# Second expert layer: rows scattered into slot order, expert matrices as moving side

## The reference, cut to what matters

```python
x = x + ffn(_layernorm(x))
# ffn, on xt = the normed tokens, 2048 x 128
logits = xt @ router_w.T                       # 8 experts
topk_vals, topk_idx = top_k(logits, 2)
g = sigmoid(topk_vals); g = g / (g.sum(-1, keepdims=True) + 1e-10)
for e in range(8):
    ge = sum(where(topk_idx == e, g, 0), -1)
    h = silu(xt @ w_gate[e]) * (xt @ w_up[e])  # 128 -> 256
    out = out + ge[:, None] * (h @ w_down[e])  # 256 -> 128
```

## Time and profile before

| | us |
|---|---|
| median of 3 executions | 437.59 |
| lowest, highest | 434.67, 439.3 |
| the profiled execution, first to last instruction (its span) | 501.4 |
| in it: start of kernel to the first gather of layer one | 54.6 |
| second layer: `slot` ready to first gather | 14.1 |
| second layer: first gather to the landing of the last scatter | 135 |

### The profile page before, as it was taken

One profiled execution on the slowest core, in us unless ns is written; L12 is line 12 of the kernel. 1 busy time (PEld: TensorE's weight loads), 2 busy tenths in 40 slices (PEclk: granted clock), 3 DMA queues, 4 the chain that ended last, 5 costly groups with the idle time before them and its releaser, 6 DMA issues. The chain is left out here.

```text
span 501.4 us, 8428 instructions
## 1 busy us (share of the span) xinstructions
PE 332.9 (66%) x2020; PEld 300.6 (60%) x2020; DVE 251.3 (50%) x890; ACT 207.0 (41%) x940; POOL 261.6 (52%) x273
## 2 busy tenths in 40 slices
PE   2669498797987878768887730723666767665630
PEld 2668387696976768668787720622556656655520
DVE  4969546544445656455565726569222322222217
ACT  4449276634445564465565501500322322232210
POOL 5996434555465466655765561302455556556530
PEclk9999899967689889898899955555787887888885
DMA  4780423222232223222342116110444443344536
GB/s 106 250 256 41 151 65 129 76 75 74 74 122 100 74 74 117 93 86 74 78 133 86 43 33 168 42 42 38 174 140 167 156 169 136 136 157 168 137 120 190
DMA packets 34694, 57.04 MB, mean 114 GB/s; under 512 B 5792, under 2 KB 21088, under 8 KB 34416
## 3 DMA queue, kind: packets, MB, share of 16 engines
q1 hardware_dynamic: 29040, 45.41, 25.3%
q0 software_dynamic: 5440, 11.15, 8.9%
q10 hardware_dynamic: 192, 0.23, 0.1%
HBM read 17.39 MB, written 8.72 MB: 52 GB/s over the span
## 5 line engine op out<-in xcount | busy, mean ns | idle before, releaser
L526 POOL DMA_INDIRECT xg<-xrows,gi x85 | 84.6, 995 | 73.1 <-issue 22.5
L538 POOL DMA_INDIRECT yrows<-yb,si x85 | 84.1, 989 | 30.0 <-issue 24.6
L549 POOL TENSOR_TENSOR rh<-c2ve,neghalf 128x8 f32<-128x8 f32 x23 | 45.8, 1991 | 77.8 <-DVE c2ve L1189 77.8
L873 PE MATMUL bank<-ident,xg 128*128 128x128 f32 x85 | 26.2, 356 | 68.9 <-DMA xg<-xrows,gi 40.5
L884 PE MATMUL bank<-wbuf,x1T 128*128 128x128 f32 x340 | 59.2, 315 | 15.6 <-DVE x1T L1239 7.8
L1236 DVE SCALAR_TENSOR_TENSOR wraw<-xn,bank 128x256 f32<-128x256 f32 x39 | 16.4, 420 | 93.9 <-ACT xn L736 66.9
L976 PE MATMUL bank<-xT,wbuf 128*128 128x128 f32 x312 | 55.8, 336 | 8.6 <-ACT xT L726 8.4
L884 PEld LDWEIGHTS bank<-wbuf,x1T 128*128 128x128 f32 x340 | 50.3, 220 | 18.6 <-issue 9.8
L892 PE MATMUL bank<-xT,wbuf 128*128 128x256 f32 x184 | 58.4, 447 | 0.5 <-ACT xT L665 0.5
L976 PEld LDWEIGHTS bank<-xT,wbuf 128*128 128x128 f32 x312 | 50.8, 247 | 11.1 <-ACT xT L726 5.2
L873 PEld LDWEIGHTS bank<-ident,xg 128*128 128x128 f32 x85 | 12.5, 172 | 74.2 <-issue 43.2
(11 more groups left out here) (180 smaller groups left out, 726.5 us busy)
## 6 DMA issues: line engine op xcount, KB each, us to landing
wbuf<-rec SPq DMA_DIRECT2D x39, 384.0 KB
wbuf<-rec SPq DMA_DIRECT2D x23, 523.0 KB
blocks<-yrows SPq DMA_DIRECT2D x8, 512.0 KB, 6.6
wbuf<-wd SPq DMA_DIRECT2D x23, 128.0 KB
wraw<-in_L_attn_w_up SPq DMA_DIRECT2D x1, 2048.0 KB, 18.5
xg<-xrows,gi POOLq DMA_INDIRECT x85
yrows<-yb,si POOLq DMA_INDIRECT x85
x<-in_L_attn_hidden_states SPq DMA_DIRECT2D x4, 256.0 KB, 4.5
```

Of the source, the lines that this page charges most:

```text
L526: g.indirect_dma_start(rows, None, xrows[l], bass.IndirectOffsetOnAxis(ap=index, axis=0)).then_inc(s_gath[l][b], 16)
L538: g.indirect_dma_start(yrows[l], bass.IndirectOffsetOnAxis(ap=index, axis=0), rows, None).then_inc(s_scat[l][b], 16)
L549: g.tensor_tensor(rh[:], c2ve[:], neghalf[:, 0:HV * NH].rearrange("p (h k) -> p h k", h=HV), ALU.pow).then_inc(s_rh, 1)
L873: ins = t.transpose(dst[:, h * P:(h + 1) * P], xg2[:, b * n + h, :], ident[:])
```

## The change

- While the first layer is being prepared, SP fills a new DRAM tensor `xslots` (39 * 128 rows of 129 words): 128 zero words and in the last word a spare destination row, different for each slot.
- The one-hot part of `route(1)` is gone. GpSimd scatters the normed rows of `x1`, now 129 words wide with the pair's number as last word, straight to their slots: 16 columns for each of 2 experts, 32 indirect DMAs.
- When all 32 have landed, SP loads tiles of 128 consecutive slots by plain DMAs into a ring of 8. The destination rows of a tile's result are the last word of the loaded rows, so no `gidx`, `sidx`, `gi2` or `si2` is used.
- The expert record is not copied. TensorE loads the expert's number into a register (twice a tile, once for gate and up, once for down) and reads `rec2` at that address as the moving side: one matmul of 512 columns for gate and up. The output has the tokens on the partitions, so before the down product the hidden tile must be turned (two transposes, and a copy by ScalarE, `hT2`).
- The loop is written out in full (44 steps) rather than a hardware loop.

```diff
+R2I, R2G, R2H, R2Y = 8, 3, 3, 4
+N2 = LNT[1]
...
# sync, before the store of xn to xrows
+            sp.wait_ge(s_fid, 2)
+            xsv = xslots.rearrange("(j p) d -> p j d", p=P)
+            sp.dma_start(xsv[:, :, 0:D], zrow[:].unsqueeze(1).to_broadcast([P, N2, D])).then_inc(s_fill, 16)
+            sp.dma_start(xsv[:, :, D:D + 1].bitcast(U32), fid[:].unsqueeze(2), allow_slow_non_contiguous=True).then_inc(s_fill, 16)
...
# sync, second layer
+            for k in range(TOPK):
+                for q in range(4):
+                    sp.wait_ge(s_disp[k][q], 64)
...
+            for j in range(N2):
+                if j >= R2I:
+                    sp.wait_ge(s_xtp[1], j - R2I + 1)
+                    sp.wait_ge(s_scat2[(j - R2I) % R2Y], 16 * ((j - R2I) // R2Y + 1))
+                sp.dma_start(xin2[:, j % R2I, :], xslots[j * P:(j + 1) * P, :]).then_inc(s_in2[j % R2I], 16)
...
# gpsimd, constants
+            g.memset(zrow[:], 0.0).then_inc(s_fid, 1)
+            g.iota(fid[:], pattern=[[P, N2]], base=PAIRS, channel_multiplier=1).then_inc(s_fid, 1)
+            for k in range(TOPK):
+                g.iota(pid[:, k, :], pattern=[[TOPK, TT]], base=k, channel_multiplier=TOPK * TT).then_inc(s_id1, 1)
...
# gpsimd, second layer
+            pool.wait_ge(s_slot, 1)
+            pool.wait_ge(s_x1[1], 4)
+            pool.wait_ge(s_fill, 32)
+            for k in range(TOPK):
+                for i in range(TT):
+                    if i % 4 == 0:
+                        pool.wait_ge(s_id1, TOPK + 1 + k * (i // 4 + 1))
+                    c = TOPK * i + k
+                    g.indirect_dma_start(
+                        xslots, bass.IndirectOffsetOnAxis(ap=slotu[:, c:c + 1], axis=0), x1[:, i, :], None)\
+                        .then_inc(s_disp[k][i // 4], 16)
+            for j in range(N2):
+                pool.wait_ge(s_yb[1], j + 1)
+                pool.wait_ge(s_in2[j % R2I], 16 * (j // R2I + 1))
+                g.indirect_dma_start(
+                    yrows[1], bass.IndirectOffsetOnAxis(ap=xin2[:, j % R2I, D:D + 1].bitcast(U32), axis=0),
+                    yb2[:, j % R2Y, :], None).then_inc(s_scat2[j % R2Y], 16)
...
# scalar: per step, xT2 of tile s+2, hT2 of s-2, tanh of s, yb2 of s-3; the last after
+                    act.wait_ge(s_y[1], j + 1)
+                    if j >= R2Y:
+                        act.wait_ge(s_scat2[j % R2Y], 16 * (j // R2Y))
+                    a.activation(yb2[:, j % R2Y, :], Y2, ACT.Copy).then_inc(s_yb[1], 1)
...
# tensor
+            def loop2(s):
+
+                if 0 <= s + 2 < N2:
+                    j = s + 2
+                    pe.wait_ge(s_in2[j % R2I], 16 * (j // R2I + 1))
+                    at_least(pe, s_xts[1], j - 1)
+                    t.transpose(XT2[j % 2], xin2[:, j % R2I, 0:D], ident[:]).then_inc(s_xtp[1], 1)
+                if 0 <= s < N2:
+                    pe.wait_ge(s_xts[1], s + 1)
+                    at_least(pe, s_hh, s - R2G + 1)
+                    e = pe.value_load(expert[1][0:1, s:s + 1], min_val=0, max_val=E - 1)
+                    t.matmul(GU2[s % R2G], xT2[:, s % R2Y, :],
+                             rec2[:, bass.ds(e, 1), GATE:GATE + 2 * I].rearrange("p a n -> p (a n)"),
+                             start=True, stop=True).then_inc(s_g, 1)
+                if 0 <= s - 2 < N2:
+                    j = s - 2
+                    pe.wait_ge(s_hh, j + 1)
+                    at_least(pe, s_hts, j - 1)
+                    for c in range(CH):
+                        ins = t.transpose(HT2[j % 2][:, c * P:(c + 1) * P], hh2[:, j % R2H, c * P:(c + 1) * P], ident[:])
+                    ins.then_inc(s_htp, 1)
+                if 0 <= s - 3 < N2:
+                    j = s - 3
+                    pe.wait_ge(s_hts, j + 1)
+                    at_least(pe, s_yb[1], j)
+                    e = pe.value_load(expert[1][0:1, j:j + 1], min_val=0, max_val=E - 1)
+                    for c in range(CH):
+                        ins = t.matmul(Y2, hT2[:, j % R2H, c * P:(c + 1) * P],
+                                       rec2[:, bass.ds(e, 1), DOWN + c * D:DOWN + (c + 1) * D].rearrange("p a n -> p (a n)"),
+                                       start=(c == 0), stop=(c == CH - 1))
+                    ins.then_inc(s_y[1], 1)
```

More of the change, by code:

```diff
@@ L126, in program @@
         hif = sb("hif", [P, TT * TOPK])
+        slotu = sb("slotu", [P, TT * TOPK], U32)
         cmpj = sb("cmpj", [1, LNT[1] + 1, E])
@@ L135, in program @@
         pairi = sb("pairi", [P, NA], U32)
-        gidx = [sb(f"gidx{l}", [P, NA], U32) for l in range(2)]
-        sidx = [sb(f"sidx{l}", [P, NA], U32) for l in range(2)]
+        gidx = [sb("gidx", [P, NA], U32)]
+        sidx = [sb("sidx", [P, NA], U32)]
         ex = sb("ex", [P, TT, TOPK])
@@ L370, in load_pairs @@
             def load_pairs(l):
-                for b in range(WAYS[l]):
-                    sp.wait_ge(s_scat[l][b], 16 * (LTS[l] // P) * ((LNT[l] - b + WAYS[l] - 1) // WAYS[l]))
+                ring, scat = ((WAYS[0], s_scat[0]), (R2Y, s_scat2))[l]
+                for b in range(ring):
+                    sp.wait_ge(scat[b], 16 * (LTS[l] // P) * ((LNT[l] - b + ring - 1) // ring))
                 yv = yrows[l][0:PAIRS, :].rearrange("(p m) d -> p m d", p=P)
@@ L526, in gather @@
                     g.indirect_dma_start(
-                        rows, None, xrows[l], bass.IndirectOffsetOnAxis(ap=index, axis=0)).then_inc(s_gath[l][b], 16)
+                        rows, None, xrows, bass.IndirectOffsetOnAxis(ap=index, axis=0)).then_inc(s_gath[l][b], 16)
             def scatter(l, u, b):
@@ L557, in _ @@
                 norms(0, quarter(c), s_rstd[1])
-            pool.wait_ge(s_used, 2)
-            paired(g)
-            for b in range(3):
-                gather(1, 0, b)
-            def step2(u, b):
-                gather(1, *earlier(1, u, b, -3))
-                scatter(1, *earlier(1, u, b, 2))
-            steps(pool, step2, 1, 2)
+            pool.wait_ge(s_slot, 1)
[15 more added lines that the diff above has]
+                    yb2[:, j % R2Y, :], None).then_inc(s_scat2[j % R2Y], 16)
         @block.scalar
@@ L745, in _ @@
+            for s in range(-2, N2 + 3):
+                loop2(s)
         @block.tensor
@@ L1061, in route @@
                         ins.then_inc(s_hot[l], 1)
[L1063 to L1067 removed]
+                experts(l)
                 dve.wait_ge(s_perm[l], 1)
@@ L1228, in _ @@
             route(1)
-            def step2(u, b):
-                if not active(1, u, b):
-                    return
-                j = 4 * u + b
-                both = bank[4 + b][:].rearrange("p (g c t) -> p g c t", g=2, c=CH)
+            for j in range(N2):
+                b = j % R2G
                 dve.wait_ge(s_thg, j + 1)
-                v.scalar_tensor_tensor(gg2[:, b], th2[:, b], 1.0, both[:, 0], ALU.add, ALU.mult).then_inc(s_gg, 1)
+                v.scalar_tensor_tensor(gg2[:, b], th2[:, b], 1.0, GU2[b][:, 0:I], ALU.add, ALU.mult).then_inc(s_gg, 1)
                 dve.wait_ge(s_gg, j + 1)
-                at_least(dve, s_y[1], j - 3)
-                v.tensor_tensor(hh2[:, b], both[:, 1], gg2[:, b], ALU.mult).then_inc(s_hh, 1)
-            steps(dve, step2, 1, 0)
+                at_least(dve, s_htp, j - R2H + 1)
+                v.tensor_tensor(hh2[:, j % R2H], GU2[b][:, I:2 * I], gg2[:, b], ALU.mult).then_inc(s_hh, 1)
             for c in range(4):
```

175 lines of the change are left out of this document (83 added, 92 removed).

## The result

The changed kernel takes 471.21 us (median of 6, 466.15 to 473.63), the kernel before 437.23 us (6 runs, 434.67 to 439.76) in the same session. The ratio is 1.0747, 95% interval 1.0677 to 1.0816: 34 us slower, where 440.4 was forecast and 464 was the upper end. The profiled execution of the changed kernel took 466.15 us, with a span of 464.4; it is the quickest of the six. On some chips every execution of these kernels is held by short stops, and the trace on which the prediction rests is of that sort (span 501.4), while the timed runs of both kernels are of the other, here called ordinary.

A forecast was written before the change was run, and what follows sets the result against it. A circle of waits was taken to hold the second layer's loop. The loop gains 32 us, the dispatch takes it back, the start adds 1.6: span +3.2 us, scaled by 0.87 to +2.8, giving 440.4 us; range 424 to 464.

The forecast's parts named there:

- the scale of 0.87: Last step of the sum: the profiled span's +3.2 us times 0.87 gives +2.8 us, 440.4 us.
- the fills: At the start: zero rows 10.2 us plus single words 2.5 us, against 11.5 us of free queue: +1.2 us.
- The circle of waits: Old second-layer loop: six indirect DMAs, last landing, then ScalarE's list hold it at 3.42 us a tile; floor 2.54.
- fills in the way: Rival at the start: words go out on one engine, store of `xn` up to 39 us later, 474 us; chance 0.07.
- The three constants: At the start: GpSimd writes three more small constants before `s_const`, all on the path: +0.4 us.
- The dispatch: Before the second loop: 32 serial scatters at 1.27 us, landing and first load; the loop begins some 28 us later.
- The rival of 1.6 us a scatter: Before the second loop: the queue limits the 32 scatters, 10 us more, 450 us; chance 0.08.
- TensorE's step: New second-layer loop: TensorE's work for one tile takes 2.0 us, or 2.7 with an exposed register load.
- The ring: New second-layer loop: row buffer reuse makes three periods one step plus 5.5 us; 2.6 us a tile taken.
- The quicker ring: Rival in the new loop: faster load, register loads hidden, 2.25 us a tile, 428 us; chance 0.25.
- The slow TensorE: Rival in the new loop: lower clock or both register loads exposed, step 3.6 to 3.9 us, 459 us; chance 0.20.
- The instruction fetch: Old second-layer loop: a 5.25 us stop fits a taken branch's forced fetch; the written-out loop would have none.

The follow-up runs named there:

- after_b: The changed kernel with no edit, run on a chip with the stops: 521.5 us against 514.42 for the kernel before, ratio 1.0157.
- hybrid_b: The changed kernel's compute loop with the old indirect gathers, ring of 16, no fills or dispatch; on chips with stops 503.45 and 503.23 us in two runs.

## Why the prediction was wrong

**The failed step: the scale of 0.87.** The prediction saw that its trace (span 501.4) was 64 us over the median, and wrote "Scaled by 0.87", as if each stage shrank alike. Its last sentence named the danger, that an ordinary execution shortens the old loop and not the serial dispatch, and said that one profile couldn't show it. This is what happened: from the last scatter of layer one to the last of layer two before takes 184.1 us in the trace read and 159.8 in an ordinary one; after takes 184.1 where 185.7 was worked out. The error of the whole sum on the new side is 1.6 us, on the old side 24.3. On the chips with stops the sum came out: +3.2 us were worked out there, +7.1 measured (ratio 1.0033 to 1.0282), and from the last scatter of layer one on, after_b takes 184.7 us where the three traces of before take 184.1 to 185.9; the rest is the fills. The scale took a surplus that the same trace put down to `remote` in two loops, 41 and 6.8 us of it, and spread it over everything.

It was also the answer to "what bounds the kernel now". The circle of waits with 2.87 us of idle GpSimd was there, but only in that sort of execution. In the ordinary one the loop is bound by GpSimd at 2.56 us a tile, which the prediction named as the floor. "So the loop gains 0.8 us a tile" became 0.1 (2.56 to 2.47).

**The fills** were mis-sized: +1.2 us was taken, 6.7 measured by the medians (7.5 to 9.2 at the first gather). The zero rows were priced at the 251 GB/s of the earlier trace rows, 10.2 us; they landed after 24.3 us, which is 105 GB/s, beside the words, whose issue alone held SP's queue for 12.56 us where 2.5 of work were assumed. Where the earlier trace rows has the DMA engines idle from 36.5 to 48, they now move 172 GB/s from 36 to 48 and 119 from 48 to 60, and the words land at 59.3. The rival (fills in the way) was right in kind, at a sixth of its 39 us; that its 474 us lie near the measured time is chance.

**The three constants** (four by the diff, with the zero row), +0.4 us, can't be seen: without early fills the first gather starts between 53.7 and 57.3 us in the traces of either kernel.

**The dispatch** was right: 32 scatters at 1.27 (1.265), landing 2.24 (2.29), SP's issue 0.14 after it (340.43 - 340.28 = 0.15), load 2.5 (1.91). The rival of 1.6 us a scatter is out. TensorE's first work lies 80.9 us behind the last scatter of layer one, 82.9 were worked out.

**TensorE's step** was given as 2.0 us, or 2.7 with an exposed register load. With two loads it is 2.21 and without any 1.60. The 2.0 had hidden loads in it: without loads it was too high by 0.4, and the loads that it put at nothing cost 0.61, so the two errors cancelled in part, which is luck. The 2.7 charged one load with 0.7; two cost 0.61.

**The ring** was right in kind and nearly in size: (step + 5.5) / 3 with the measured step of 2.21 is 2.57, measured 2.47; the value taken was 2.6. With the measured load (1.91, near the 2.0 of the quicker ring) and landing the 5.5 are 5.0 and the formula gives 2.40. The quicker ring's 2.25 didn't come, as its step of 1.8 had the loads at nothing. That the ring and not the step is the bound is shown by the ring of 16, in which the period falls to the step's 2.21.

**The slow TensorE** didn't come: the clock is 0.95 in the new loop, 0.65 in its first 7.6 us, behind the dispatch at 0.50, and 0.98 from 350 us on. By the Trainium skill (TensorE: Matmul & The Clock Gate, Part 1), a TensorE that waits between bursts falls back to half clock, and the prediction left open whether the new loop's short waits would do. In this trace they don't: short waits are in the new loop in nearly every step (0.52 us before L1014). Behind the long wait of the dispatch it does agree.

**The instruction fetch.** The 5.25 us stop was put beside the rule of the Trainium skill (Runtime: NRT & Kernel Launch, Instruction fetch mechanics), that straight code is fetched ahead. No run bears this out as the cause: on a chip without stops the looped code of before has no such stop in its chain, and on a chip with stops the written-out loop with gathers (hybrid_b) still has 8.9 us of them under ScalarE's copy of the result. What the written-out loop of the changed kernel lacks is more than the branch, so the rule is neither shown nor refuted, but the stops go with the chip and with the gathers, not with the form of the loop.

**The chances.** Slower had 0.45, the direction with the most weight, but as a mixture of rivals none of which is what happened: that the direction came true is no merit of the working.

## What to carry to other kernels

If the profiled execution is longer than the timed ones, don't scale it: look in the list of waits of the whole span for releasers that are nothing of the kernel, and in which stage they lie, ask of each wait whether it would survive in a shorter execution, and cost the change once with the loop as read and once with it at its floor. A change that keeps the floor can't gain more than the loop's distance from it; one that removes it, as here the gathers, is bounded by the next engine. The serial stage on GpSimd was paid in full on both sorts of chip (39.2 us from its first scatter to its last). And a register load in TensorE's queue was cheapest behind a long matmul that is already issued, once for each tile; its cost shows in the period and only in part in the idle rows, so measure it by replacing it with a constant.

## What the runs showed that was not expected

**Two sorts of chips.** The kernel before took 514 to 516 us on two chips and 436 to 438 on three others, each execution within 3% of its chip's median. On the first two the waits list the `remote` releaser that the ordinary traces don't have; of the changed kernel there (after_b):

```profile
DVE h L1275 <- remote: 25.1, 14, 3.1
ACT pre L706 <- remote: 12.8, 7, 2.5
DVE nig L1207 <- remote: 6.9, 2, 3.7
```

Its traces on the other chips have none. The granted clock is also lower there (0.79 over the span of before, against 0.89 on an ordinary chip), but a stop needs no fall: from 100 to 120 us of after_b the clock was full, and yet

```profile
102.93 0.48 DVE L1275 SCALAR_TENSOR_TENSOR h<-bank,onib,wraw 128x256 f32<-128x256 f32 x1 [2.43 <-remote]
```

The stops fall in loops with gathers (the first layer of every kernel, the second of before and of the one with gathers) and not in the changed kernel's second loop, whose period is 2.47 us on either sort of chip. What they are stays open: the traces with them show no landing times for most transfers of those loops, so the releaser can't be read.

**A fill of 4992 rows in one DMA** landed after 24.3 us and one of 4992 single words took SP 12.56 us to issue and landed after 26.4; the next store in the same queue then took 7.05 us to issue and 13.1 to land.

**The register loads** of TensorE: two in a step cost 0.61 us with long work between them, one behind a 1.02 us matmul cost nothing that the period shows (1.60 with it and with constants).
